# Layer-0 FFN of a four-layer Flamingo stack on one NeuronCore: the picked experts' first matrices gathered from HBM by indirect DMA instead of copied from a table in SBUF

## The chip, the cores and the metric

The kernel is one program on one core of one Trainium2 chip. The metric is the device time in microseconds of one execution; the time before is the median of 3 runs. The engines are named as in the profile: PE is TensorE (its weight loads are PEld), DVE is VectorE, ACT is ScalarE, POOL is GpSimd, SP is SyncE, which issues nearly all DMA transfers. A trailing q (DVEq, POOLq, SPq) marks the engine's own instruction queue.

## The reference

The input x is 16 batches of 256 tokens of 128 numbers, in fp32. Four layers follow each other, each a gated cross-attention and a gated FFN on layer-normed x. The change touches the FFN of layer 0, which picks two of eight experts for each batch (not for each token) from the mean of its tokens:

```python
def _L0_ffn_ref(x, gate_w, down_w, down_b, up_w, up_b):
    pooled = x.mean(axis=1)
    gate = jax.nn.softmax(pooled @ gate_w.T, axis=-1)
    top_w, top_i = jax.lax.top_k(gate, 2)
    top_w = top_w / (top_w.sum(axis=-1, keepdims=True) + 1e-08)
    Wd, bd, Wu, bu = down_w[top_i], down_b[top_i], up_w[top_i], up_b[top_i]
    h = gelu(einsum('bsd,bkcd->bksc', x, Wd) + bd[:, :, None, :])
    h = h * top_w[:, :, None, None]
    out = einsum('bksc,bkdc->bsd', h, Wu)
    return out + (top_w[:, :, None] * bu).sum(axis=1)[:, None, :]
...
x = x + jnp.tanh(g_ffn[0]) * _L0_ffn_ref(_layernorm(x, axis=-1), ...)
```

`pooled` is (16, 128), `down_w` is (8, 64, 128): one picked expert's first matrix is 64x128 fp32, 32 KB, and the 16 batches pick 32 of them.

## The kernel before

The program is written by hand, one instruction stream for each engine, tied together by semaphores: no scheduler moves anything, each engine executes its stream in order, and an instruction that waits holds back all behind it. x stays in SBUF for the whole kernel, as 32 tiles of 128 tokens. Attention is a software pipeline over the tiles (`attention(a)` gives a `step` for each engine; step t works on tiles t-3 to t+4). The opening steps -5, -4 and -3 of layer 1's attention are woven into the end of layer 0's FFN (`OPENING_BATCH = {12: -5, 13: -4, 14: -3}`).

**The routing of layer 0's FFN** is a chain of small DVE instructions (`route(...)`, lines 1071 to 1103), each waiting for the one before it by the semaphore `route_step`. The first index of the top two of each batch is kept in reversed form (8 minus the expert's number) in `T12 = lg[0:16, 3, 2:4]`, one batch to a partition. When the second pick is there (`ROUTE["picked0"]`), PE transposes the two columns into one row of `GV` (line 1572), behind `keep_busy(WARM_PICKS, ...)`, 14 matmuls of 128x128 on constants whose results nobody reads. DVE goes on with the gates (line 1090 to 1100), PE transposes the gates (line 1576), ACT copies them out (L807), PE makes the biases and the gates as columns for each batch, ACT copies those out (`w0col`, L809), and PE fills the wait with 6 more such matmuls (`WARM_COLUMNS`). At line 1103 DVE turns the row of picks into integers (`picks0`, `f0_idx`).

**The weights.** `wd_all` (128x512) holds all eight first matrices side by side, transposed so that the partition is the input channel d; SP loads it in line 415 early in the program. After `f0_idx`, POOL reads the picks of two batches into four registers (L618) and copies each picked 128x64 block into `wd_sel[:, b, :]` (L621), 32 copies, the two of a batch side by side: one matmul then handles both experts. DVE does the like for the second matrices, scaled by the gate (`up_weights`, L1117).

**The batches.** PE runs `up0(b)` (one matmul of 128x256, waits for `wd_made`, the weights of batch b) and `down0(b)` (three matmuls into PT). `up0` runs three batches ahead: up0(0), up0(1), up0(2), then for each b up0(b+3) and down0(b). ACT applies Gelu between the two (L816), DVE adds the result into x (`add0`, L1123). Behind the 32 copies, POOL's stream goes on with the opening of layer 1's attention: for tile 0 it waits for `mv_done`, which DVE gives behind `add0(12)`.

SP loads the attention weights of layer 2 (1.8 MB) in the middle of this stage, as soon as the values of layer 1 are made and `wq1` is copied.

Of the kernel before, what the change touches and what calls it, by code (L numbers as in the profile page):

```python
# [22 lines left out]
I32 = mybir.dt.int32  # L23
ALU = mybir.AluOpType
ACT = mybir.ActivationFunctionType
AX = mybir.AxisListType
ds = bass.ds

P = 128
BATCHES = 16  # L30
SEQ = 256
D = 128
# [6 lines left out]
EXPERTS = 8  # L39
BN = 64  # L40
# [35 lines left out]
class Signals:  # L76


    def __init__(self, sem):
# [70 lines left out]
        self.table_warm = sem("table_warm")  # L150
        self.wd_made = sem("wd_made")
        self.wu_made = sem("wu_made")
# [98 lines left out]
def flamingo_program(nc, io):  # L251
    with ExitStack() as ctx:
        def sb(name, shape, dt=F32):
            return ctx.enter_context(nc.sbuf_tensor(name, shape, dt))
# [10 lines left out]
        GV = ps("GV", [P, BANK])  # L265
# [30 lines left out]
        ident = sb("ident", [P, P])  # L296
# [37 lines left out]

        wd_all = sb("wd_all", [P, EXPERTS * BN])
        wd_sel = arena[:, 2048:4096].rearrange("p (b c) -> p b c", b=BATCHES)
# [64 lines left out]
        s = Signals(sem)  # L401
# [11 lines left out]
        def _(sp):  # L413
            def load(dst, src, sm):
                sp.dma_start(dst, src).then_inc(sm, 16)
# [46 lines left out]

            load(wd_all[:, :], io["L0_down_T"], s.f0_loaded)
            for n in range(2):
# [29 lines left out]
        def _(pool):  # L494
# [10 lines left out]
                      allow_small_or_imprecise_dtypes=True).then_inc(s.consts_made, 1)  # L505
            pool.wait_ge(s.consts_made, 9)
            pool.affine_select(out=ident[:, :], in_=ident[:, :], compare_op=ALU.not_equal, fill=1.0, base=0,
# [106 lines left out]
            pool.wait_ge(s.f0_loaded, F0)  # L614
            pool.wait_ge(s.f0_idx, 1)
            picked = [pool.alloc_register(f"down_pick{n}") for n in range(4)]
            for b in range(0, BATCHES, 2):
                pool.load(picked, picks0[0:1, b:b + 2, :].rearrange("p b k -> p (b k)"))  # L618
                for n in range(4):
                    e = pool.snap(picked[n], min_val=0, max_val=EXPERTS - 1)  # L620
                    ins = pool.tensor_copy(wd_sel[:, b + n // 2, BN * (n % 2):BN * (n % 2) + BN], wd_all[:, ds(e * BN, BN)])  # L621
                    if n % 2:
                        ins.then_inc(s.wd_made, 1)
            pool.wait_ge(s.m_evac, ATTN[2].mn0)
# [307 lines left out]
        def _(dve):  # L932
# [114 lines left out]
            def at(name):  # L1047

                assert ROUTE[name] == route_count[0], (name, route_count[0])

# [36 lines left out]
            route(dve.scalar_tensor_tensor(out=A0, in0=B0, scalar=second, in1=rv, op0=ALU.is_equal, op1=ALU.mult))  # L1087
            route(dve.tensor_reduce(T12[:, 1:2], A0, AX.X, ALU.max))
            at("picked0")
            route(dve.tensor_scalar(two, A0, T12[:, 1:2], None, ALU.is_equal))  # L1090
            dve.wait_ge(s.f0_exp, 2)
# [238 lines left out]
        def _(pe):  # L1330
# [239 lines left out]
            pe.wait_ge(s.route_step, ROUTE["picked0"])  # L1570
            for k in range(2):
                ins = pe.transpose(GV[0:1, 16 * k:16 * k + 16], lg[0:16, 3, 2 + k:3 + k], ident[0:16, 0:16])
            ins.then_inc(s.f0_picks_T, 1)
# [15 lines left out]
            def up0(b):  # L1589
                pe.wait_ge(s.wd_made, b + 1)  # L1590
                done(pe, s.act0_done, b - 4)
                mm(S[b // 2 % 2][:, BANK * (b % 2):BANK * (b % 2) + SEQ], wd_sel[:, b, :], xnT[:, SEQ * b:SEQ * b + SEQ]).then_inc(s.up0_done, 1)
# [140 lines left out]
SMALL = 11 * 16  # L1733
F0 = 5 * 16

WARM_UP, WARM_WEIGHTS, WARM_MN, WARM_DRAIN = 8, 2, 6, 2
WARM_POOLED, WARM_PICKS, WARM_COLUMNS = 4, 14, 6

ROUTE = {"pooled": 1, "exp0_ready": 3, "second0_ready": 8, "picked0": 10, "gates0": 20, "exp1_ready": 33, "exp2_ready": 42}
Q3 = {"inverses": 6, "weights": 10, "x_scale": 3, "h_scale": 3 + GROUPS + 2}  # L1740
# [38 lines left out]
```

## Time and profile before

| | |
|---|---|
| median of 3 runs | 1340.53 us (1340.12 to 1344.09) |
| the profiled execution | 1344.25 us, span from first to last instruction 1342.5 us |
| PE busy | 1242.9 us (93%) |
| DVE, ACT, POOL busy | 1044.0, 615.7, 562.1 us |
| mean granted TensorE clock | 0.965 |
| DMA | 15.36 MB, 11 GB/s over the span |
| layer 0's FFN, from the pooled means to `add0(15)` | 159.5 to 204.3 us of the span |

The profile counts an engine busy while an instruction of its own runs; a wait is put down to the engine and line that ended it. The granted clock is 1.00 at 2.4 GHz and 0.50 at 1.2 GHz. PE records of an fp32 matmul come in twos, so "x8" of `up0` is four matmuls.

### The profile page before, as it was taken

What the parts mean: (1) busy time and instruction counts of PE and PEld (TensorE: products, weight loads), DVE (VectorE), ACT (ScalarE), POOL (GpSimd) and SP (SyncE); (2) the same over time, 40 slices, a digit from 0 to 9 for tenths busy, and PEclk for the clock granted to TensorE, in tenths of its full rate; (3) what the DMA queues carried; (4) which work ended last, traced back from release to release, by engine and by line L of the source; (5) the groups of instructions that cost most, each with busy time, mean ns of one, the idle gap of its engine ahead of it and who ended that gap; (6) DMA issues with size and microseconds to landing.
All of it is one profiled execution on the core that took longest, in us unless ns stands there. A gap on an engine that the chain in (4) does not pass through costs nothing.

```text
span 1342.5 us, 25933 instructions
## 1 busy us (share of the span) xinstructions
PE 1242.9 (93%) x7491; PEld 912.2 (68%) x7492; DVE 1044.0 (78%) x2366; ACT 615.7 (46%) x1286; POOL 562.1 (42%) x1007
## 2 busy tenths in 40 slices
PE   7999788999998899999999998999999999999843
PEld 5666554666667788876766766888887666766612
DVE  3999556999996777777777775777776998888777
ACT  3555323555554322235555554322223555555475
POOL 2666324666675011315445543001001666666413
PEclk8999998999999899999999998999999999999975
DMA  8100200000000200000000000000000000000002
GB/s 215 49 0 1 55 2 1 1 0 0 0 1 1 55 1 0 0 0 1 1 0 0 0 1 1 1 1 0 0 0 1 1 1 0 0 0 1 1 0 63
DMA packets 24352, 15.36 MB, mean 11 GB/s; under 512 B 3833, under 2 KB 23074, under 8 KB 24290
## 3 DMA queue, kind: packets, MB, share of 16 engines
q1 hardware_dynamic: 24290, 14.59, 4.2%
q8 instruction: 32, 0.52, 0.2%
q14 instruction: 30, 0.25, 0.1%
HBM read 12.49 MB, written 2.10 MB: 11 GB/s over the span
## 4 chain that ended last, share of the span: by engine, by line
PE 74%; DVE 5%; ACT 5%; issue 4%; POOL 2%; ACTq 0%; DVEq 0%; POOLq 0%
PE S L1332 29%; PE OX L1332 14%; PE GV L1332 12%; PE PT L1332 11%; PE PT L1501 5%; ACT pT L780 1%; PE OX L1449 1%; POOL arena L565 1%; PE OX L1452 1%; ACT arena L760 1%; DVE arena L1275 1%; ACT moe_flat L893 1%; DVE zsum L1010 1%; POOL x L662 0%; DVE arena L1305 0%
## 5 line engine op out<-in xcount | busy, mean ns | idle before, releaser
L1332 PEld LDWEIGHTS OX<-arena,pT 128*128 128x128 f32 x1792 | 211.4, 193 | 55.0 <-issue 32.7
L565 POOL TENSOR_TENSOR arena<-arena,zinv 128x1024 f32<-128x1024 f32 (+1 forms) x128 | 215.9, 1687 | 75.5 <-DVE zinv L1014 75.4
L1332 PE MATMUL OX<-arena,pT 128*128 128x128 f32 x1792 | 231.8, 281 | 9.2 <-ACT pT L780 6.5
L831 ACT ACTIVATE arena<-S 128x512 f32<-128x512 f32 x144 | 86.0, 597 | 236.5 <-PE S L1332 236.5
L994 DVE TENSOR_REDUCE nmax<-S 128x16 f32<-128x1024 f32 (+1 forms) x128 | 139.7, 1092 | 47.6 <-PE S L1332 39.3
L1173 DVE TENSOR_TENSOR arena<-S,arena 128x512 f32<-128x512 f32 x144 | 99.6, 692 | 84.5 <-ACT arena L831 81.0
L1181 DVE SCALAR_TENSOR_TENSOR x<-PT,gate,x 128x128 f32 (+1 forms) x576 | 161.0, 343 | 2.2 <-PE PT L1332 2.2
L1332 PE MATMUL S<-arena,xT 128*128 (+1 forms) x320 | 161.0, 601 | 1.1 <-ACT arena L760 0.8
L537 POOL TENSOR_TENSOR rstd<-mv,eps 128x1 f32<-128x1 f32 x128 | 24.5, 192 | 315.1 <-DVE mv L996 315.1
L1003 DVE TENSOR_TENSOR arena<-S,nmax 128x1024 f32<-128x1024 f32 (+1 forms) x128 | 138.1, 1079 | 0.0
L1010 DVE TENSOR_REDUCE zsum<-arena 128x16 f32<-128x1024 f32 (+1 forms) x128 | 137.5, 1075 | 0.0
L1501 PEld LDWEIGHTS PT<-ident,arena 128*128 128x128 f32 x896 | 99.9, 142 | 51.8 <-issue 27.0
L1332 PE MATMUL S<-xh,w_low 128*128 (+1 forms) x288 | 126.1, 438 | 7.2 <-issue 7.2
L780 ACT ACTIVATE pT<-PT 128x512 f32<-128x512 f32 x224 | 123.6, 597 | 19.0 <-PE PT L1501 18.3
L1501 PE MATMUL PT<-ident,arena 128*128 128x128 f32 x896 | 125.2, 280 | 6.5 <-POOL arena L565 6.3
L727 ACT ACTIVATE arena<-arena 128x1024 f32<-128x1024 f32 (+1 forms) x128 | 120.7, 943 | 14.3 <-DVE arena L1003 14.3
L975 DVE TENSOR_SCALAR xn<-x,mv,rstd 128x128 f32 (+1 forms) x128 | 118.9, 929 | 8.0 <-POOL rstd L559 3.7
L1332 PE MATMUL GV<-N,ctx_b 97*64 97x512 f32 x448 | 122.1, 623 | 1.9 <-ACT arena L770 1.4
L586 POOL CAST xh<-xnT (+1 forms) x16 | 10.2, 636 | 252.5 <-PE S L1332 248.3
L1332 PE MATMUL S<-xh,w_high 128*128 (+1 forms) x288 | 114.2, 397 | 0.0
L1332 PE MATMUL S<-xl,w_high 128*128 (+1 forms) x288 | 113.4, 394 | 0.0
L770 ACT ACTIVATE arena<-GV 128x512 f32<-128x512 f32 x112 | 67.0, 598 | 83.0 <-PE GV L1332 82.9
(258 smaller groups left out, 2174.3 us busy)
## 6 DMA issues: line engine op xcount, KB each, us to landing
x<-in_x SPq DMA_DIRECT2D x4, 512.0 KB, 7.8
out<-x SPq DMA_DIRECT2D x8, 256.0 KB, 2.3
moe_flat<-in_L_ffn_w SPq DMA_DIRECT2D x3, 512.0 KB, 7.1
arena<-in_L_xattn_Wq SPq DMA_DIRECT2D x2, 512.0 KB
wo_in<-in_L_xattn_Wo SPq DMA_DIRECT2D x2, 512.0 KB
moe_flat<-in_L_up_T SPq DMA_DIRECT2D x2, 256.0 KB
moe<-in_L_ffn_we_gate SPq DMA_DIRECT2D x1, 512.0 KB, 5.3
moe<-in_L_ffn_we_up SPq DMA_DIRECT2D x1, 512.0 KB, 6.7
```

Source lines behind the costliest of these rows:

```text
L565: pool.tensor_tensor(pr, pr, z, ALU.mult).then_inc(s.probs_done, 1)
L727: act.activation(pr, pr, ACT.Exp).then_inc(s.exp_done, 1)
L780: act.activation(pT[:, r % 2, BANK * k:BANK * k + BANK], PT[:, BANK * k:BANK * k + BANK], ACT.Copy).then_inc(s.turned_evac, 1)
L831: act.activation(silu[:, e % 2, :], S[0][:, BANK * (e % 2):BANK * (e % 2) + BANK], ACT.Silu).then_inc(s.silu_done, 1)
L975: dve.tensor_scalar(xn2[:, r % 2, :], tokens(t - 2), mv2[:, q, 0:1], rstd2[:, q, 1:2], ALU.subtract, ALU.mult).then_inc(s.xn2_done, 1)
L994: dve.tensor_reduce(nmax[:, p, 0:H], sc, AX.X, ALU.max, negate=True).then_inc(s.max_done, 1)
L1003: dve.tensor_tensor(probs[:, j, 0:W].rearrange("p (h k) -> p h k", h=H), sc, nmax[:, p, 0:H].unsqueeze(2).to_broadcast([P, H, KEYS]), ALU. ...
L1010: dve.tensor_reduce(zsum[:, p, 0:H], probs[:, j, 0:W].rearrange("p (h k) -> p h k", h=H), AX.X, ALU.add).then_inc(s.sum_done, 1)
L1173: dve.tensor_tensor(hid[:, e % 2, :], S[1][:, BANK * (e % 2):BANK * (e % 2) + BANK], silu[:, e % 2, :], ALU.mult).then_inc(s.hid_done, 1)
L1181: ins = dve.scalar_tensor_tensor(out=xt, in0=PT[:, BANK * (e % 2) + P * q:BANK * (e % 2) + P * q + P], scalar=gate[:, ds(4 * g + q, 1), e: ...
L1332: return pe.matmul(out, lhsT, rhs, start=start, stop=stop)
L1501: ins = pe.transpose(PT[:, o:o + P], probs[:, r, o:o + P], ident[:, :])
```

## The change

The table `wd_all` and its load are gone. The first matrices lie in HBM as 1024 rows of 64 numbers (row 128*e + d), and each of the 32 copies on POOL becomes an indirect DMA from HBM: 128 rows of 256 bytes, one index for each partition, from a column of `rows0` (128x32, integers). To make `rows0`, DVE spreads the two columns of picks over diagonals (two instructions more in the routing chain), PE multiplies them by ones, which gives every partition all 32 picks (`GV[:, 32:64]`), and DVE turns them into row numbers with the partition's number (`row_base`, an iota made by POOL at the start). Each batch has a semaphore of its own, which both its transfers raise by 16.

```diff
-        self.wd_made = sem("wd_made")
+        self.wd_made = [sem(f"wd_made{b}") for b in range(BATCHES)]
+        self.f0_rows = sem("f0_rows")
+        self.f0_rows_T = sem("f0_rows_T")
...
-        wd_all = sb("wd_all", [P, EXPERTS * BN])
+        rows0 = sb("rows0", [P, 2 * BATCHES], I32)
+        row_base = sb("row_base", [P, 1])
...
-            load(wd_all[:, :], io["L0_down_T"], s.f0_loaded)
...
+            pool.iota(row_base[:, :], pattern=[[0, 1]], base=8 * P, channel_multiplier=1,
+                      allow_small_or_imprecise_dtypes=True).then_inc(s.consts_made, 1)
...
-            pool.wait_ge(s.f0_idx, 1)
-            picked = [pool.alloc_register(f"down_pick{n}") for n in range(4)]
-            for b in range(0, BATCHES, 2):
-                pool.load(picked, picks0[0:1, b:b + 2, :].rearrange("p b k -> p (b k)"))
-                for n in range(4):
-                    e = pool.snap(picked[n], min_val=0, max_val=EXPERTS - 1)
-                    ins = pool.tensor_copy(wd_sel[:, b + n // 2, BN * (n % 2):BN * (n % 2) + BN], wd_all[:, ds(e * BN, BN)])
-                    if n % 2:
-                        ins.then_inc(s.wd_made, 1)
+            pool.wait_ge(s.f0_rows, 1)
+            for b in range(BATCHES):
+                for k in range(2):
+                    n = BATCHES * k + b
+                    pool.indirect_dma_start(wd_sel[:, b, BN * k:BN * k + BN], None, io["L0_down_T"],
+                                            bass.IndirectOffsetOnAxis(ap=rows0[:, n:n + 1], axis=0)).then_inc(s.wd_made[b], 16)
...
+            for k in range(2):
+                route(dve.tensor_scalar(ra[0:16, 4 + 2 * k:6 + 2 * k, :].rearrange("p a e -> p (a e)"), ident[0:16, 0:16], T12[:, k:k + 1], None, ALU.mult))
             at("picked0")
+            dve.wait_ge(s.f0_rows_T, 1)
+            dve.tensor_scalar(rows0[:, :], GV[:, 32:64], -float(P), row_base[:, :], ALU.mult, ALU.add).then_inc(s.f0_rows, 1)
             route(dve.tensor_scalar(two, A0, T12[:, 1:2], None, ALU.is_equal))
...
             pe.wait_ge(s.route_step, ROUTE["picked0"])
             for k in range(2):
+                ins = mm(GV[:, 32 + 16 * k:48 + 16 * k], ones[0:16, :], ra[0:16, 4 + 2 * k:6 + 2 * k, :].rearrange("p a e -> p (a e)"))
+            ins.then_inc(s.f0_rows_T, 1)
+            pe.wait_ge(s.f0_rows, 1)
+            for k in range(2):
                 ins = pe.transpose(GV[0:1, 16 * k:16 * k + 16], lg[0:16, 3, 2 + k:3 + k], ident[0:16, 0:16])
...
-                pe.wait_ge(s.wd_made, b + 1)
+                pe.wait_ge(s.wd_made[b], 32)
```

`F0` goes from 5 * 16 to 4 * 16, and the later marks of `ROUTE` rise by two.

On POOL, between the copy of `wq1` and the opening of layer 1's attention, before the change (the first rows of 72; `TENSOR_LOAD` fills the registers, the `ISA` row stands ahead of each copy):

```order
L611 COPY M<-arena 128x128 [waits attn_w_loaded,g_done]
L618 TENSOR_LOAD picks [waits f0_idx,f0_loaded,out_done]
L620 ISA
L621 COPY arena<-wd_all 128x64
L620 ISA
L621 COPY arena<-wd_all 128x64
```

and after it:

```order
L615 COPY M<-arena 128x128 [waits attn_w_loaded,g_done]
L623 DMA arena<-in_L_down_T,rows 128x64 [waits f0_rows,f0_loaded,out_done]
L623 DMA arena<-in_L_down_T,rows 128x64 x31
L541 TENSOR_TENSOR rstd<-mv,eps 128x1 [waits mv_done,mn_done,m_evac]
L544 TENSOR_TENSOR rstd<-rstd,neg_half 128x1 [waits rstd_step]
```

The 32 transfers stand back to back in POOL's stream, and the opening of attention is behind all of them.

On DVE, the end of the routing chain before the change (`rb` and `oh` are scratch of the routing, `lg` holds `T12`):

```order
L1087 SCALAR_TENSOR_TENSOR rb<-rb,m,rev 16x8 [waits route_step]
L1088 TENSOR_REDUCE lg<-rb 16x1 [waits route_step]
L1090 TENSOR_SCALAR oh<-rb,lg 16x8 [waits route_step]
L1092 SCALAR_TENSOR_TENSOR r<-r 16x1 [waits f0_exp,route_step]
```

and after it:

```order
L1089 SCALAR_TENSOR_TENSOR rb<-rb,m,rev 16x8 [waits route_step]
L1090 TENSOR_REDUCE lg<-rb 16x1 [waits route_step]
L1092 TENSOR_SCALAR ra<-ident,lg 16x16 [waits route_step] x2
L1095 TENSOR_SCALAR rows<-GV,row_base 128x32 [waits f0_rows_T,route_step]
L1096 TENSOR_SCALAR oh<-rb,lg 16x8
L1098 SCALAR_TENSOR_TENSOR r<-r 16x1 [waits f0_exp,route_step]
```

Three instructions stand ahead of L1096 (`two`), and the third waits for PE.

On PE, after the change, from the matmuls that keep it busy to the transposes of the gates:

```order
L1338 MATMUL S<-ones 128x128 x14
L1338 MATMUL GV<-ra,ones 128x16 [waits route_step]
L1338 MATMUL GV<-ra,ones 128x16
L1582 MATMUL GV<-ident,lg 1x16 [waits f0_rows]
L1582 MATMUL GV<-ident,lg 1x16
L1586 MATMUL PT<-ident,oh 8x16 [waits route_step]
```

The first transpose of the picks now waits for `rows0`, where it waited for the picks alone.

## Rows read from the trace of the kernel before

**Rows 1.** The page: busy time of each engine.

```profile
PE 1242.9 (93%) x7491; PEld 912.2 (68%) x7492; DVE 1044.0 (78%) x2366; ACT 615.7 (46%) x1286; POOL 562.1 (42%) x1007
```

**Rows 2.** Chain that ended last, 168 to 195 us: start us, us, what.

```profile
170.94 1.26 PE PT L1332 x6
172.20 0.43 PE S L1332 x2
172.63 1.26 PE PT L1332 x6
173.90 0.43 PE S L1332 x2
...
191.33 1.28 PE PT L1332 x6
```

**Rows 3.** Timeline, PE: start us, us, engine line op, out<-in, count, idle before.

```profile
162.30 0.21 PE L1332 MATMUL OX<-gwT,pooled 128*16 128x8 f32 x2
162.44 3.39 PE L1332 MATMUL S<-ones 128*128 128x128 f32 x28
165.76 0.20 PE L1572 MATMUL GV<-ident,lg 16*1 16x16 f32 x2
...
169.04 1.89 PE L1332 MATMUL S<-xnT,arena 128*128 128x256 f32 x8
...
190.73 0.60 PE L1332 MATMUL S<-xnT,arena 128*128 128x256 f32 x2
```

**Rows 4.** Timeline, DVE, end of the routing chain.

```profile
162.62 0.15 DVE L1078 TENSOR_REDUCE m<-OX 16x1 f32<-16x8 f32 x1 [2.90 <-PE OX L1332]
...
164.49 0.22 DVE L1090 TENSOR_SCALAR oh<-rb,lg 16x8 f32<-16x8 f32 x1
...
166.21 0.48 DVE L1100 TENSOR_SCALAR ra<-ident,lg 16x16 f32<-16x16 f32 x2
166.72 0.18 DVE L1103 TENSOR_SCALAR picks<-GV 1x32 int32<-1x32 f32 x1
```

**Rows 5.** Timeline, POOL: the copies and what is behind them.

```profile
167.74 5.95 POOL L621 COPY arena<-wd_all 128x64 f32 x28 [10.98 <-DVE picks L1103]
174.07 0.77 POOL L621 COPY arena<-wd_all 128x64 f32 x4 [0.38 <-issue]
193.78 0.19 POOL L537 TENSOR_TENSOR rstd<-mv,eps 128x1 f32<-128x1 f32 x1 [18.94 <-DVE mv L996]
```

**Rows 6.** Groups by line and form, POOL: the copies.

```profile
L621 POOL COPY arena<-wd_all 128x64 f32 x32 | 6.3, 240 | 11.8 <-DVE picks L1103 11.0 <-issue 0.4
```

**Rows 7.** Timeline, SPq: how long the issue of a DMA takes.

```profile
12.60 2.69 SPq L415 DMA_DIRECT2D bo_in<-in_L_xattn_bo  x3
15.33 0.43 SPq L415 DMA_DIRECT2D ln_g<-in_L_xattn_ln_gamma  x1
15.81 0.43 SPq L415 DMA_DIRECT2D ln_b<-in_L_xattn_ln_beta  x1
...
25.21 1.71 SPq L415 DMA_DIRECT2D router_w<-in_L_ffn_router_w  x1
```

**Rows 8.** DMA issues: count, KB each, median us from issue to landing.

```profile
q_in<-in_L_ffn_w_up SPq DMA_DIRECT2D x1, 128.0 KB, 2.4
...
wvT<-in_L_v_T SPq DMA_DIRECT2D x1, 48.5 KB, 2.7
```

**Rows 9.** Windows: busy us of each engine, granted clock, DMA share, GB/s.

```profile
core 0: us, PE busy (x) PEld busy (x) DVE busy (x) ACT busy (x) POOL busy (x), PEclk, DMA share, GB/s
166.00:168.00 2.00, 0.97 (x14) 0.83 (x15) 0.80 (x4) 0.46 (x3) 0.26 (x2) 1.00 0.72 177
195.00:197.00 2.00, 0.31 (x1) 0.18 (x1) 1.93 (x3) 0.00 (x0) 1.65 (x2) 0.50 0.00 0
206.00:210.00 4.00, 3.35 (x8) 0.78 (x6) 1.78 (x3) 0.88 (x2) 0.31 (x2) 0.71 0.00 0
218.00:225.00 7.00, 5.73 (x34) 3.52 (x33) 6.18 (x11) 3.28 (x6) 3.53 (x5) 1.00 0.00 0
```

**Rows 10.** Timeline, PE, behind the last `up0`.

```profile
196.69 0.45 PE L1449 MATMUL OX<-ident,xn 128*128 128x128 f32 x1 [2.83 <-DVE xn L1023]
...
200.29 1.22 PE L1332 MATMUL PT<-arena 128*128 128x128 f32 x4
201.44 1.22 PE L1332 MATMUL PT<-upb_in,w0T 8*128 8x256 f32 x2
```

**Rows 11.** One line: POOL's all-reduce near the end, and what it waited for.

```profile
L650 POOLq MODIFY_POOL_CONFIG  x4: 11/11/11, 1271.6 to 1301.1; - x4
L650 POOL PARTITION_ALL_REDUCE gmax<-amax x2: 378/380/382, 1277.4 to 1314.9; - x2
...
issue: 5.7, 1
```

More of the change, by code:

```diff
@@ L505, in _ @@
                       allow_small_or_imprecise_dtypes=True).then_inc(s.consts_made, 1)
-            pool.wait_ge(s.consts_made, 9)
+            pool.iota(row_base[:, :], pattern=[[0, 1]], base=8 * P, channel_multiplier=1,
+                      allow_small_or_imprecise_dtypes=True).then_inc(s.consts_made, 1)
+            pool.wait_ge(s.consts_made, 10)
             pool.affine_select(out=ident[:, :], in_=ident[:, :], compare_op=ALU.not_equal, fill=1.0, base=0,
@@ L1733 @@
 SMALL = 11 * 16
-F0 = 5 * 16
+F0 = 4 * 16
 WARM_UP, WARM_WEIGHTS, WARM_MN, WARM_DRAIN = 8, 2, 6, 2
 WARM_POOLED, WARM_PICKS, WARM_COLUMNS = 4, 14, 6
-ROUTE = {"pooled": 1, "exp0_ready": 3, "second0_ready": 8, "picked0": 10, "gates0": 20, "exp1_ready": 33, "exp2_ready": 42}
+ROUTE = {"pooled": 1, "exp0_ready": 3, "second0_ready": 8, "picked0": 12, "gates0": 22, "exp1_ready": 35, "exp2_ready": 44}
 Q3 = {"inverses": 6, "weights": 10, "x_scale": 3, "h_scale": 3 + GROUPS + 2}
@@ L1765 @@
         "L1_v_T": np.concatenate([np.asarray(inputs["L1_xattn_wv"]), np.asarray(inputs["L1_xattn_bv"])[None, :]], axis=0).T,
-        "L0_down_T": np.asarray(inputs["L0_ffn_down_w"]).transpose(2, 0, 1).reshape(D, EXPERTS * BN),
+        "L0_down_T": np.asarray(inputs["L0_ffn_down_w"]).transpose(0, 2, 1).reshape(EXPERTS * D, BN),
         "L0_up_T": np.asarray(inputs["L0_ffn_up_w"]).transpose(2, 0, 1).reshape(BN, EXPERTS * D),
```

## The prediction
> **What bounds the kernel now.** I read the page first: PE is busy 93% of the span, POOL 42% [rows 1]. That share says nothing of this stage, so next the chain that ended last, cut to the stage: from 170.94 us on it is PE alone, in a beat of two pieces, six records into PT (`down0`) at 1.26 us and two into S (`up0`) at 0.43 us [rows 2]. The reader should see the regularity: 1.70 us for each batch, with no wait in between. PE sets the pace, and the copies on POOL don't: by POOL's timeline they run from 167.74 to 174.84 us, 7.1 us for all 32, and then POOL stands idle for 18.94 us until DVE gives it the statistics of tile 0 [rows 5]. A weight block for each batch every 0.44 us is far ahead of a PE that wants one every 1.70 us. The stage begins with the first `up0` at 169.04 and its last one, `up0(15)`, starts at 190.73 [rows 3]. Everything behind that (down0(12), the opening of layer 1) hangs on it. So the question is when `up0(15)` can start after the change.
>
> **The front of the stage.** DVE had the second pick at 164.49, where `two` began [rows 4]. Two instructions of 16x16 are put ahead of it; the pair of the same shape took 0.48 us [rows 4], so the diagonals are ready at about 165.0. PE isn't: its 14 matmuls on constants run from 162.44, and the next instruction began at 165.76 [rows 3]. The two products with ones go there; the two small transposes at that place took 0.20 us [rows 3]. PE to DVE costs 0.1 us (162.30 plus 0.21 on PE, 162.62 on DVE [rows 3, 4]). So `rows0` starts at 166.07, takes 0.18 like `picks0` [rows 4], and is there at 166.25.
>
> Two things follow. First, DVE stands still meanwhile, and the gates are queued behind it: `two` starts at 166.3 instead of 164.49, 1.8 us late. PE's transposes of the gates, ACT's copies, the gate columns and the 6 matmuls in front of `up0(0)` all wait for that chain, and up0(0) can't start before 169.04 + 1.8 = 170.8. Second, POOL gets its order earlier: the first gather starts at 166.35, where the first copy began at 167.74 [rows 5].
>
> The loads of registers on POOL and the copies, 7.1 us, are removed: worth nothing, since POOL waited 18.94 us behind them [rows 5]; that idle time is also the only cover for what replaces them. The load of `wd_all` goes: nothing, as it is on nobody's chain. The iota on POOL at the start is one small instruction among some fifteen, covered by PE's first matmuls: nothing.
>
> **The gathers.** All 32 stand back to back in POOL's stream. The trace of before has no transfer issued by POOL, so their price g (POOL's time for each) has to be bounded. From below: an issue on SP, done by hardware, 0.43 us, at a distance of 0.48 us from the next [rows 7]. From above: the longest issue of one transfer on SP, 1.71 us for `router_w` [rows 7]. The nearest row is `bo_in`: a transfer to 128 partitions, one short row each, 2.69 us for three, 0.90 each [rows 7]. POOL has to read 128 indices as well, and one pass of POOL over 128x64 takes 0.24 us [rows 6]. I add the two and take g = 1.1 us, 35.2 us for 32. This is halfway between the two ends, and I keep 0.48 and 1.71 for the range.
>
> The landing: a small load takes 2.4 to 2.7 us from issue to landing [rows 8], of which 0.43 is the issue; I take 2.0 us behind POOL's instruction (bounds 1.9 and 2.7). The first gathers also meet the weights of layer 2, which still kept the DMA engines busy at a share of 0.72 from 166 to 168 us [rows 9]; that delays the first blocks, not the last.
>
> The Trainium skill speaks against such a price: "DMA: Bandwidth & Descriptors", section "Anatomy of one DMA", says that most of the fixed 2 us of such a transfer is the receipt of the last byte and that many descriptors can be emitted before their cost shows. By that rule the gathers would overlap and g would be small; the result would be that of rival A below. No row here shows it either way. The same page's "Latency and other measured facts" gives about 1 us to the first byte for transfers generated on GpSimd, and with g = 1.0 the sum below would come to 9.6 us, an estimate by that page.
>
> **The sum.** Batch b has its two blocks at 166.35 + 2.2(b+1) + 2.0. Two blocks a batch need 2.2 us against PE's 1.70 [rows 2], so the bound passes from PE to POOL. up0(0) is ready at 170.55, just ahead of its 170.8. But PE runs `up0` three batches ahead, so down0(0) stands behind up0(3), which waits until 177.2. `up0(15)` can start at 166.35 + 35.2 + 2.0 = 203.55. Before, it started at 190.73 [rows 3]: **+12.8 us**. PE's 0.5 us of slack per batch can't be used, and its 1.8 us late start is inside the wait. Behind up0(15) the same things follow as before: POOL is free at 201.55, ahead of the statistics of tile 0 (they need add0(12), some 2 us behind up0(15)), so its opening isn't late on its own account. The layers after it are moved as a block.
>
> The profiled execution took 1344.25 us, 3.7 above the median of the runs shown; against itself it would be 1357.1. On the median, 1340.53 + 12.8 = **1353.3 us**.
>
> **The rivals.**
>
> *A: the gathers are hidden after all.* The issue on POOL is as cheap as on SP, 0.48 us [rows 7]. A batch then needs 0.96 us, PE keeps the bound at 1.70, and all that is left is the late start, 1.8 us: 1342.3, no change that can be measured. For it: the page's rule above, and POOL's idle 18.94 us. Against it: POOL computes addresses for 128 rows in software, and its cheapest pass over 128 partitions with a computed result costs half of that already. This decides where 166.35 + 32g + 2.0 falls below 194.7, so below g = 0.82. For a gain nothing speaks: PE's chain, not the weights, set the beat.
>
> *B: the gathers are dear.* g lies at the upper end, 1.71 us [rows 7]: 166.35 + 54.7 + 2.0 = 223.1, +32.3 us, 1372.8. With DVE instructions sharing SBUF with POOL, or indices costing more than a pass, g of 1.3 to 1.5 is well possible (+19.2 and +25.6). PE would then be idle for 1.3 us of each 3.0.
>
> *C: the clock falls.* Waiting for the first four blocks (170.8 to 177.2) PE has 0.43 us of work in each 2.2. Behind an idle stretch of 2.83 us [rows 10] the granted clock stood at 0.50, 1.2 GHz, and it had come back only between 206 and 210 [rows 9]. At that level six records into PT took 1.22 + 1.22 us [rows 10] instead of 1.26, so a batch costs about 3.3 us, more than the gathers' 2.2, and PE is the bound again. If it stayed so to the end: 177.2 + 12 x 3.3 = 216.8, +26.1, 1366.6. If it comes back within some batches, PE catches up at 0.5 us a batch and nothing is lost but perhaps 2.5 us, when the last batches still run at half clock (1355.8). PE at 82% was granted 1.00 from 218 to 225 [rows 9]; here it would be busy 77%.
>
> *D: POOL must first load code.* The all-reduce near the end came 5.7 us after a MODIFY_POOL_CONFIG in which it waited for nothing else [rows 11]. Were the first gather to pay this, the whole series is later: +18.5, 1359.0. The skill's "GPSIMD Engine Reference" names about 6 us for a first call to freshly loaded code; the trace's 5.7 agrees. Against it: the order of the changed kernel shows no such row ahead of the gathers.
>
> *E: the change doesn't do what it says*, the transfers being issued but something else holding `up0`: the waits are plain in PE's stream, 0.01.
>
> **How the numbers follow.** A measurement of this kernel tells 0.3%, 4.0 us, from no change. Forecast (g from 0.9 to 1.3, clock back soon) 0.60, at 1347 to 1360; A 0.07; B (g over 1.3) 0.17; C held to the end 0.10; D 0.05; E 0.01. The range takes in the forecast, C, D and B up to g of 1.5: 1346 to 1368, leaving out A and the dear end of B. Slower by over 0.3%: 0.92; within 0.3%: A with E, 0.07; faster 0.01.
>
> **What would show it.** Right: POOL's queue has 32 transfers back to back of 1.1 us each from 166.4 to about 201.6; in PE's timeline the beat of `up0` is 2.2 us with idle time before `up0`, released by a DMA; `two` (L1096) starts near 166.3; the last `up0` near 203.6. The stages behind keep their lengths. Wrong: the beat stays 1.70 (A), a gap of 6 us ahead of the first gather (D), or PE back to back at a granted clock of 0.50 (C).

## The result, and the profile of the changed kernel

| | before | changed |
|---|---|---|
| median, us | 1340.57 (4 runs) | 1386.91 (4 runs, 1385.95 to 1388.8) |
| profiled execution: span, us | 1342.5 | 1384.2 |
| mean granted clock | 0.965 | 0.941 |

The changed kernel is slower by 46.3 us; the ratio is 1.0328, 95% interval 1.0311 to 1.0345. The prediction was 1353.3 us: the direction was right, and the loss was more than three times the +12.8 forecast and lay outside the range (1346 to 1368).

The page first: PE's share fell, POOL's didn't. That is all it says of this stage.

```profile
PE 1264.4 (91%) x7496; PEld 922.5 (67%) x7496; DVE 1041.7 (75%) x2369; ACT 614.4 (44%) x1286; POOL 585.0 (42%) x1008
```

POOL's timeline answers to [rows 5]: first gathers and last one, and the first work behind them.

```profile
168.06 1.29 POOL L623 DMA_INDIRECT arena<-in_L_down_T,rows  x1 [10.96 <-DVE rows L1095]
169.66 0.94 POOL L623 DMA_INDIRECT arena<-in_L_down_T,rows  x1 [0.30 <-issue]
...
207.11 0.94 POOL L623 DMA_INDIRECT arena<-in_L_down_T,rows  x1 [0.30 <-issue]
239.44 0.18 POOL L541 TENSOR_TENSOR rstd<-mv,eps 128x1 f32<-128x1 f32 x1 [31.39 <-DVE mv L998]
```

The beat is 0.94 + 0.30 = 1.25 us, and the 32 gathers take 168.06 to 208.05. POOL then stands idle for 31.39 us. So POOL isn't what set the end, and PE's timeline has to be read (it answers to [rows 3]):

```profile
166.11 0.61 PE L1338 MATMUL GV<-ra,ones 16*128 16x16 f32 x4
...
169.38 0.21 PE L1586 MATMUL PT<-ident,oh 16*8 16x16 f32 x2 [2.04 <-DVE ra L1106]
...
173.18 1.06 PE L1338 MATMUL S<-xnT,arena 128*128 128x256 f32 x2
...
179.64 1.22 PE L1338 MATMUL S<-xnT,arena 128*128 128x256 f32 x2 [1.24 <-DMA arena<-in_L_down_T,rows]
...
192.42 1.06 PE L1338 MATMUL S<-xnT,arena 128*128 128x256 f32 x2
208.86 1.19 PE L1338 MATMUL PT<-upb_in,w0T 8*128 8x256 f32 x2 [15.38 <-issue]
...
213.84 1.19 PE L1338 MATMUL PT<-upb_in,w0T 8*128 8x256 f32 x2 [1.79 <-DVE x L1129]
...
234.90 1.06 PE L1338 MATMUL S<-xnT,arena 128*128 128x256 f32 x2
```

`up0(15)` starts at 234.90 instead of 190.73: +44.2 us, which is nearly the whole loss. (The two profiled spans differ by 41.7 us only: in the later layers the distance between the same instructions shrinks to some 40 us, first in the stretches of 200 us where the granted clock was 0.98 after and 0.97 before.) Three things are to be seen: `up0(3)` waits for its block until 179.64; from there a batch takes 3.15 us, not 1.70; and PE stands still for 15.38 and 1.79 us.

The windows give the clock: busy time of each engine, with PEclk behind it.

```profile
core 0: us, PE busy (x) PEld busy (x) DVE busy (x) ACT busy (x) POOL busy (x), PEclk, DMA share, GB/s
170.00:180.00 10.00, 7.03 (x27) 4.84 (x28) 2.84 (x10) 3.10 (x6) 7.56 (x9) 0.50 0.11 29
180.00:190.00 10.00, 10.00 (x26) 5.70 (x25) 1.67 (x5) 0.95 (x2) 7.56 (x9) 0.50 0.09 27
190.00:200.00 10.00, 3.48 (x9) 1.85 (x8) 0.29 (x2) 0.47 (x1) 7.56 (x9) 0.50 0.10 26
...
220.00:230.00 10.00, 10.00 (x26) 5.98 (x26) 3.25 (x11) 1.73 (x4) 0.00 (x0) 0.50 0.00 0
```

PE is at 1.2 GHz throughout, also where it is busy for 10.00 of 10.00 us. And DVE's timeline shows what PE stood still for:

```profile
189.39 0.42 DVE L1129 TENSOR_TENSOR x<-PT,x 128x256 f32<-128x256 f32 x1 [5.02 <-remote]
189.73 0.57 DVE L1123 TENSOR_SCALAR arena<-moe_flat,w0col 64x128 f32 x2
208.29 0.42 DVE L1129 TENSOR_TENSOR x<-PT,x 128x256 f32<-128x256 f32 x1 [17.99 <-remote]
...
213.27 0.42 DVE L1129 TENSOR_TENSOR x<-PT,x 128x256 f32<-128x256 f32 x1 [3.89 <-remote]
```

```profile
213.20 1.20 ACT L818 ACTIVATE arena<-S,w0col 128x256 f32<-128x256 f32 x3 [19.12 <-PE S L1338]
```

The `add0` at 208.29 is batch 2's. Its `down0(2)` was over on PE at about 189.5, so DVE had nothing to wait for and yet waited 17.99 us; "remote" means that the view finds no instruction near it in time that released it. ACT's gelu waited 19.12 us in the same way, until 213.20. PE's next `down0` needs that `add0` and stopped in turn. The signals from DVE to PE were prompt (208.71 to 208.86); those from PE were not. The lag outlasted the gathers: the last one was over at 208.05, `add0` of batch 2 came 0.24 us behind it, but ACT's three waiting gelus and `add0` of batch 3 (over on PE at about 192.5) came only at 213.2, and that is PE's second wait, of 1.79 us. The profile's ends of matmuls are modelled, so the trace can't tell whether only the signal was late or the end of the matmul itself. I call this **the stop**.

By sizes, at `up0(15)`: the gathers alone would have put it at 208.05 + 1.7 (landing, from an experiment below) = 209.75, +19.0. At half clock it is 179.64 + 12 x 3.15 = 217.4, another 7.7. The stop adds 15.38 + 1.79 = 17.2. The sum is 43.9 of the 44.2. No run has the gathers alone at full clock, so the first term is an estimate from these rows; experiment 14 below has the second, 38.0 us from `up0(3)` to `up0(15)` without a stop.

### The profile page after: what moved, and what is told of

Read it like the earlier page. It is cut to its first block and busy times, and to the rows that moved or that the text cites. A ratio compares the mean times of both kernels' runs of the same rounds, so it can differ in the third digit from the quotient of the medians.

```text
span 1384.2 us, 25906 instructions
## 1 busy us (share of the span) xinstructions
PE 1264.4 (91%) x7496; PEld 922.5 (67%) x7496; DVE 1041.7 (75%) x2369; ACT 614.4 (44%) x1286; POOL 585.0 (42%) x1008
## 3 DMA queue, kind: packets, MB, share of 16 engines
q0 software_dynamic: 1024, 1.05, 0.3%
```

## The experiments

**1. Gathers that nobody waits for.** Before, with gathers behind its copies:

```diff
+            for n in range(12):
+                pool.indirect_dma_start(spare[:, n, :], None, io["L0_down_T"]...,
+                                        bass.IndirectOffsetOnAxis(ap=row_i[:, 0:1], axis=0)).then_inc(s.spare, 16)
+            pool.wait_ge(s.spare, 12 * 16)
```

> The kernel before, with 12 indirect transfers of 128 rows added on POOL behind its 32 copies, with constant indices and into a spare part of the arena that nobody reads; POOL alone waits for them before its opening of layer 1. This is gathers beside the batches with nothing waiting for their data. The trace of the changed kernel has g = 1.25 us a gather, so 12 take 15.0 us behind the copies (about 174.9 to 190), and POOL was idle until 193.78 there. Theory 'stall' (gathers hold back the signals between PE, ACT and DVE while they run): DVE's add0 and ACT's gelu get late by several us at about 180 to 190, PE waits for them, and the time is 1345 to 1356 us. Theory 'clock alone' (the 15.4 us stop of PE in the changed kernel has another cause, such as the half clock or the order of waits): nothing moves in the batches, up0(15) stays at 190.7 within 0.5 us, and the time is that of before, 1340.5 within 1.5.

Measured: 1349.86 us against 1343.41, ratio 1.0050 (1.0032 to 1.0067). DVE's `add0` in this kernel, one per batch, should come every 1.70 us:

```profile
182.52 0.42 DVE L1135 TENSOR_TENSOR x<-PT,x 128x256 f32<-128x256 f32 x1 [0.74 <-PE PT L1344]
185.09 0.42 DVE L1135 TENSOR_TENSOR x<-PT,x 128x256 f32<-128x256 f32 x1 [1.47 <-PE PT L1344]
190.03 0.42 DVE L1135 TENSOR_TENSOR x<-PT,x 128x256 f32<-128x256 f32 x1 [3.99 <-remote]
```

The first gather was at 176.37; 9 us later PE's signals begin to lag, and this at a granted clock of 1.00 (until 191.4). No data of a gather was awaited. So gathers hold up PE's signals, and the half clock isn't needed for it.

**2. PE filled with narrow matmuls.**

```diff
             ins.then_inc(s.f0_picks_T, 1)
+            keep_busy(16, S[1])
...
             def up0(b):
+                keep_busy(16 if b < 4 else 7, OX)
                 pe.wait_ge(s.wd_made[b], 32)
```

> The changed kernel with PE filled by matmuls on constants into a bank nobody reads: 16 behind the transposes of the picks, 16 ahead of each of the first four up0 and 7 ahead of each later one, so that PE is not idle while it waits for gathers. At full clock one takes about 0.06 us, so the fillers fit into the wait of the gathers' beat of 2.5 us. Theory 'clock alone': the granted clock stays at 1.00 through the batches, the beat becomes the gathers' 2 x 1.25 = 2.5 us, up0(15) starts at about 168.06 + 32 x 1.25 + 1.2 = 209.3, and the time is 1340.5 + 18.6 = 1359 us (1355 to 1364). Theory 'stall': the clock is held, but PE still waits 10 to 16 us near 195 to 208 for a signal of ACT or DVE; up0(15) comes at 215 to 225 and the time is 1366 to 1376. If matmuls on constants do not hold the clock, it stays near 1387.

Measured: 1416.30 us, ratio 1.0539 (1.0517 to 1.0562), outside all three ranges. One filler took 0.24 us, not 0.06: 14 of them show as 28 records and took 3.39 us, and I had counted badly, so the fillers alone slow the batches. But the trace tells more. PE's timeline and windows, while POOL gathers:

```profile
193.26 0.37 PE L1338 MATMUL OX<-ones 128*128 128x128 f32 x1 [1.74 <-issue]
...
199.55 0.37 PE L1338 MATMUL OX<-ones 128*128 128x128 f32 x1 [1.52 <-issue]
201.67 0.37 PE L1338 MATMUL OX<-ones 128*128 128x128 f32 x1 [1.74 <-issue]
204.46 0.37 PE L1338 MATMUL OX<-ones 128*128 128x128 f32 x1 [2.42 <-issue]
```

```profile
190.00:200.00 10.00, 3.00 (x7) 1.74 (x7) 0.00 (x0) 0.00 (x0) 7.56 (x9) 0.50 0.09 27
...
220.00:230.00 10.00, 10.00 (x75) 8.62 (x75) 0.99 (x3) 1.42 (x3) 0.00 (x0) 1.00 0.00 1
```

These matmuls wait for no semaphore and send none, and still PE runs one record, half a matmul, in some 2 us (11 records from 190.43 to 210.06): beside the gathers PE itself is held back, not only its signals. The clock accounts for a factor of two, not for this. The two records of `up0(0)` started at 177.89 and 179.09, and ACT got its signal at 214.33. From 220 us on, with the gathers over, 75 records fit into 10 us.

**3. All gathers ahead of the batches.**

```diff
             pe.wait_ge(s.wq1_copied, 1)
+            for b in range(BATCHES):
+                pe.wait_ge(s.wd_made[b], 32)
```

> The changed kernel with PE waiting for all 32 gathers before up0(0): no batch overlaps a gather. The last block is there at about 209.3. Theory 'stall' (overlap of gathers with the batches is what stops PE): from there no wait of PE for DVE or ACT; up0(15) follows 12 batches after up0(3), at 1.70 us each at full clock about 230.5, at 3.15 us at half clock about 248. Time 1340.5 + 39.8 = 1380 or + 57 = 1398. Theory that the stop of 15 us has to do with the half clock and not with the gathers: a stop of over 5 us appears in this kernel too, behind the gathers, and the time is over 1400.

Measured: 1402.09 us (four runs, 1385.6 to 1404.9), ratio 1.0403 (1.0329 to 1.0477). There is no stop, so it needs the overlap. The last gather ended at 207.53 and `up0(0)` began at 209.23, 1.7 us behind it: the landing. And the clock:

```profile
212.00:250.00 38.00, 38.00 (x98) 22.39 (x97) 10.41 (x33) 5.69 (x12) 0.00 (x0) 0.50 0.00 0
```

38 us of batches without a gap, and the clock stays at 0.50. This is the case with half clock that the expectation named (1398 us), and it explains the profiled execution (1400.96). The run of 1385.6 has the highest mean granted clock of the four, 0.947 against 0.931 to 0.939; it has no profile.

**4. The front alone.** Before's copies behind the changed routing front, nobody gathers:

```diff
-                    pool.indirect_dma_start(wd_sel[:, b, ...], ..., rows0[:, n:n + 1] ...).then_inc(s.wd_made[b], 16)
+                    ins = pool.tensor_copy(wd_sel[:, b + n // 2, ...], wd_all[:, ds(e * BN, BN)])
```

> The changed kernel's routing front (the two diagonals, the products with ones, rows0, and PE and DVE waiting for one another there), but the blocks copied on POOL from the resident table by registers, as before; nobody reads rows0. It prices the front alone. By the prediction's step the front costs 1.8 us (2.5 by the changed kernel's trace, of which 0.35 lies ahead of it), up0(0) at 170.8 to 171.5, 1342.3 to 1343.0 us, if the clock is granted back as it was before. Theory 'the front starts the fall of the clock': PE is idle for 2.0 us ahead of the gates' transposes, the granted clock falls to 0.50 from 169 on, and the batches run at 3.15 us for as long as it is held: +10 to +24 us, 1350 to 1365. Theory 'the waits for the gathers start it': clock 1.00 through the batches, 1342 to 1344 us.

Measured: 1347.36 against 1343.41 us, ratio 1.0022 (1.0010 to 1.0034). That lies between the two ranges. The clock did fall, in the 1.91 us of idle PE ahead of the gates' transposes (at 168.8), but it came back at 175.7:

```profile
170.00:176.00 6.00, 5.98 (x28) 5.42 (x28) 3.08 (x10) 2.67 (x6) 5.18 (x26) 0.53 0.00 1
176.00:196.00 20.00, 20.00 (x95) 12.10 (x94) 10.42 (x33) 5.60 (x12) 1.26 (x7) 1.00 0.01 2
```

So the front starts the fall and costs about 4 us. Here the first three `up0` ran at half clock and the batches went on at 1.00 all the same. That the waits for gathers are what kept the clock down in the changed kernel is likely (in experiments 10 and 14 it came back in the front and fell again behind such waits), but not shown: in experiment 3 it stayed at 0.50 with no wait in the batches.

**5. Hardware transfers instead of gathers.** Before, without copies; SP fetches the picked blocks from memory, by registers, from the table in HBM as it lies before the change (rows of 256 bytes, 2 KB apart):

```diff
+                    for b in range(0, BATCHES, 2):
+                        sp.load(picked, picks0[0:1, b:b + 2, :].rearrange("p b k -> p (b k)"))
+                        for n in range(4):
+                            e = sp.snap(picked[n], min_val=0, max_val=EXPERTS - 1)
+                            sp.dma_start(wd_sel[:, b + n // 2, BN * (n % 2):BN * (n % 2) + BN],
+                                         io["L0_down_T"][:, ds(e * BN, BN)]).then_inc(s.wd_made[b + n // 2], 16)
```

> The kernel before, with the picked first matrices fetched from memory too, but issued by SP: SP loads the picks into registers, as POOL did, and issues 32 ordinary transfers of 128 rows whose source column comes from a register, in the place in its order behind layer 2's weights. No copies on POOL, no indirect transfer, no product with ones and no wait in the front. The nearest rows of SP: 0.48 us from issue to issue, 0.90 each for bo_in's 128 rows. Theory 'software transfers' (the delay of PE's signals comes from POOL writing its transfers' descriptors): no signal of PE comes late; with 0.48 a transfer PE keeps the pace and the time is 1341 to 1345; with 0.9 each, the last block is at about 167.7 + 29 + 2 = 199 us, +8 us, 1347 to 1352 (up to 1362 if the clock falls in the wait for the first blocks). Theory 'any small rows' (128 rows of 256 bytes from memory beside PE do it, whoever issues them): a stop of over 5 us in the batches here too, and 1365 or more.

Measured: ten runs, of which two took 1345.5 and 1346.0 us and eight 1363.9 to 1367.6; their median is 1365.2, but no single figure fits both. The mean granted clock of the two was 0.963 and 0.966, of the eight 0.944 to 0.950. (The table is still loaded in this kernel, but nobody reads it.) The profile is of one of the eight. It has no stop, and most of its loss is clock:

```profile
168.58 20.38 SPq L490 DMA_DIRECT2D arena<-in_L_down_T  x32
```

```profile
173.86 0.70 PE L1333 MATMUL S<-xnT,arena 128*128 128x256 f32 x2 [1.18 <-DMA arena<-in_L_down_T]
```

```profile
176.00:196.00 20.00, 20.00 (x52) 11.65 (x51) 5.66 (x18) 2.88 (x7) 0.00 (x0) 0.50 0.17 37
```

An issue costs 0.64 us, 1.27 a batch, so PE keeps the bound; `up0(3)` was only 4 us late. But idle stretches of 0.81, 0.34, 1.18 and 0.27 us ahead of the first four `up0` were followed by 0.50 from 175.6 to 230.2: 12 batches of 3.15 us instead of 1.70, `up0(15)` at 212.24, +21.5, of which the clock is some 17.

**6. Plain transfers issued by POOL.** The first experiment with

```diff
-                pool.indirect_dma_start(spare[:, n, :], None, ...)
+                pool.dma_start(spare[:, n, :], io["L0_down_T"][:, BN * (n % 8):BN * (n % 8) + BN]).then_inc(s.spare, 16)
```

> The first experiment's kernel with its 12 indirect transfers on POOL replaced by 12 plain ones of the same shape (128 rows of 256 bytes at fixed addresses, same place in POOL's order, same target). The indirect ones cost +6.5 us and made ACT's gelu and DVE's add0 4.5 us late at about 190. Theory 'software transfers': POOL spends about 1 us on each of these too, and PE's signals come late: 1344 to 1351. Theory 'the indices': plain transfers are cheap and disturb nobody, 1340 to 1343.5.

Measured: 1343.80 against 1343.19 us, ratio 1.0000 (0.9986 to 1.0014).

```profile
177.96 6.78 POOL L633 DMA_DIRECT2D arena<-in_L_down_T  x12 [1.06 <-issue]
```

0.57 us each, and every `add0` from 175.97 to 189.56 came 1.70 us behind the last. As many bytes to the same partitions, issued by the same engine, disturb nobody, and it isn't the DMA engines' load: from 180 to 184 us these transfers moved 0.25 MB at a mean share of 25.6%, the gathers of the first experiment 0.10 MB at 8.2%. Two things differ besides the form. The source rows lie 2 KB apart here and side by side there. And the series is over in 6.8 us, while in the first experiment the lag began only 9 us behind the first gather. Experiment 5 had 32 plain transfers over 20 us without a stop, but from SP. So the indirect form is the likely cause; a plain series of 15 us on POOL was not run.

**7. Gathers with pauses.** The first experiment with six gathers and, behind each,

```diff
+                pool.memset(spare[:, 6:16, :], 0.0).then_inc(s.pace, 1)
+                pool.wait_ge(s.pace, n + 1)
```

> The first experiment's kernel with half the gathers (6) and a memset of POOL with its own signal between any two (0.5 to 1 us), so that the series lasts nearly as long but POOL issues at about half the rate or a bit more. Theory 'backlog' (while a gather runs PE's signals drain more slowly than the batches make them, and the lag adds up): with pauses PE's signals can drain; no add0 is over 1 us late and the time is 1340 to 1343.5. Theory 'any gather stops the others for a fixed time': half the loss, 1343 to 1345, and late signals in this trace too.

Measured: 1343.84 against 1343.19 us, ratio 1.0000 (0.9988 to 1.0012), beat 1.88 us, no `add0` more than half a microsecond late. Six may have been too few, so the pauses were tried in the changed kernel too (10 and 14).

**8. PE filled with wide matmuls.**

```diff
+                fill_wide(3 if b < 4 else 1, OX)     # 128x384 each
```

> The changed kernel with PE filled as in the second experiment, but by matmuls of 384 columns: 3 in the front, 3 ahead of each of the first four up0, 1 ahead of each later one, so about the same busy time with a fifth of the added instructions (24 instead of 164). Theory 'backlog by instructions' (what is held up beside the gathers goes with the number of PE's instructions): PE is stopped for much less than in the filled kernel (1416 us), though for more than 10 us, since the batches' own 13 instructions remain; 1370 to 1395. Theory 'backlog by PE's busy time': as the filled kernel, 1405 to 1420. Theory that the stop was of the narrow fillers' own making and the clock is all else: 1359.

Measured: 1390.30 us, ratio 1.0337 (1.0308 to 1.0366).

```profile
170.00:186.00 16.00, 15.79 (x72) 10.49 (x72) 2.96 (x10) 3.27 (x7) 12.23 (x13) 1.00 0.09 28
```

```profile
196.62 1.19 PE L1338 MATMUL PT<-upb_in,w0T 8*128 8x256 f32 x2 [10.30 <-issue]
...
214.11 1.19 PE L1338 MATMUL PT<-upb_in,w0T 8*128 8x256 f32 x2 [13.02 <-ACT arena L818]
```

The clock stayed at 1.00 up to the stop, and the stop came all the same, 23.3 us in two parts. By its time the kernel falls to the theory of instructions (1370 to 1395), not to that of busy time. But between the first gather and the point where PE stuck stood 80 matmul records here, in 18 us; 87 in 10.5 us with the narrow fillers; 63 in 25.4 us in the changed kernel; and 56 in 11.7 us in the first experiment. Neither count is the same in all four, so what sets the moment of the stop stays open.

**9. Before, with its own idle stretch filled.**

```diff
+                    if a.l == 1 and isinstance(t, int) and t == -3:
+                        keep_busy(20, S[0])
                     if is_tile(t + 3):
                         pe.wait_ge(s.xn_done, a.tile0 + t + 4)
```

> The kernel before with 20 matmuls on constants (0.13 us each, 2.7 us) in PE's idle stretch of 2.83 us ahead of the transpose of tile 0 in layer 1's opening, so that the idle stretch behind which the granted clock fell to 0.50 (194.7 to 208.3 and again 211.7 to 215.2 us) is gone. Theory 'idle PE loses the clock': 1.00 is kept over this place, the pieces that took 1.22 us there take 0.7, and the 10 us of PE's work done at half clock take 5 less: 1335.5 us (1333 to 1338). Theory that the fall has another cause, or that the fillers only delay the transpose: 1340 to 1343.

Measured: 1342.54 against 1343.65 us, ratio 0.9996 (0.9986 to 1.0006), no difference. The 20 took 4.63 us, pushed the transpose back by some 1.5 us, and the clock fell later, from 202.7 to 209.4.

**10. The changed kernel with a pause behind each gather.**

```diff
+                    pool.memset(arena[:, 6528:7168], 0.0).then_inc(s.pace, 1)
+                    pool.wait_ge(s.pace, 2 * b + k + 1)
```

> The changed kernel with POOL pausing behind each gather by a memset of 128x640 with its own signal, which in the 6 spaced gathers made a beat of 1.88 us instead of 1.25 with no signal of PE late. It makes the gathers themselves slower: the last lands at about 168.1 + 32 x 1.88 + 1.2 = 229.5, where the changed kernel's up0(15) started at 234.9. Theory 'backlog' (gathers back to back, not their number, hold up PE's signals): no stop of PE other than for the blocks, up0(15) at 229.5 to 231, so about 4 us faster than the changed kernel in spite of 20 us more of POOL's time: 1379 to 1384. Theory 'number' (the six were too few to show it): the stop of 15 us is here too, 1395 or more.

Measured: 1381.72 us, ratio 1.0293 (1.0273 to 1.0313), where the changed kernel has 1.0328 (1.0311 to 1.0345).

```profile
184.56 1.22 PE L1341 MATMUL S<-xnT,arena 128*128 128x256 f32 x2 [2.59 <-DMA arena<-in_L_down_T,rows]
...
207.00 1.22 PE L1341 MATMUL S<-xnT,arena 128*128 128x256 f32 x2 [0.32 <-DMA arena<-in_L_down_T,rows]
...
229.30 1.22 PE L1341 MATMUL S<-xnT,arena 128*128 128x256 f32 x2
```

32 gathers, 20 us more of POOL's time, no stop, and faster. The number of gathers isn't the cause. The clock had come back at 176.1 and fell again at 179.5: a wait of 1.37 us for a block lay behind PE, and it was in one of 2.99 us.

**11. SP's transfers, with PE filled.**

```diff
             def up0(b):
+                if b < 4:
+                    keep_busy(6, OX)
```

> The kernel that fetches the picked matrices by SP's hardware transfers, with 6 matmuls on constants (0.8 us) ahead of each of the first four up0, where PE waited 0.81, 0.34, 1.18 and 0.27 us for blocks. Its ten runs without them fell into two groups: two at 1345.5 to 1346.0 and eight at 1364 to 1367.6, and in the profiled one (1365.0) the clock fell to 0.50 at 175.8 and stayed until 230.4 with PE never idle. Theory 'the half clock, once there, holds itself through the batches, and short idle stretches ahead of them start it': with PE filled all runs are in the fast group, 1343 to 1347 us, and the clock is 1.00 from 166 to 194 us. Theory that the two groups have another cause: both groups again.

Measured: six runs, 1348.9 to 1352.3, median 1351.41 against 1343.65 us, ratio 1.0065 (1.0050 to 1.0080). One group of times, clock 1.00 from 166 to 203.6; the time is above the 1343 to 1347 expected, because the fillers were too long (6 us in all).

**12. Before, with fewer fillers** (11 in place of 20).

> The kernel before with 11 matmuls on constants instead of the 20 of the last try ahead of the transpose of tile 0. In that run one took 0.23 us (4.63 for 20), not the 0.13 counted; two records make one matmul. The 20 delayed the transpose by 1.5 us and the clock still fell, later and for half as long (203.1 to 209.9). With 11 (2.5 us) the transpose isn't delayed. Theory 'the half clock is what the stretch costs': 1.5 to 4 us faster than before, ratio 0.997 to 0.999. Theory 'the fall only moves': no difference, ratio 0.999 to 1.001.

Measured: 1340.63 against 1342.51 us (12 and 22 runs), ratio 0.9984 (0.9971 to 0.9997). Windows over the opening, before and this kernel:

```profile
194.00:216.00 22.00, 16.11 (x35) 7.00 (x35) 8.47 (x14) 5.62 (x11) 6.13 (x9) 0.61 0.00 1
```

```profile
194.00:216.00 22.00, 17.61 (x65) 8.95 (x66) 10.96 (x18) 6.20 (x12) 6.98 (x12) 0.84 0.00 0
```

The median is 1.9 us below the kernel before, and the interval just leaves out no difference: a small gain, and the only one here.

**13. SP's transfers with 2 fillers each.**

> The kernel that fetches by SP's hardware transfers with 2 matmuls (0.5 us) instead of 6 (1.5 us each time) ahead of each of the first four up0. With 6 the clock held in the profiled run and all six runs were in one group, but up0(15) started at 197.8, since the fillers alone took 6 us: 1351.4. With 2 they fit into the waits for the blocks: up0(3) at about 174.9, up0(15) at 195.3, +4.6 us at most, 1343.5 to 1347.5 and one group of runs, if so much filling is enough to keep the clock; two groups, the slow one near 1365, if not.

Measured: 1347.92 against 1342.51 us (11 runs, 1344.5 to 1350.8), ratio 1.0038 (1.0025 to 1.0050), one group, 0.4 us above the range expected.

```profile
176.00:196.00 20.00, 20.00 (x96) 12.24 (x95) 10.84 (x34) 4.84 (x11) 0.00 (x0) 1.00 0.16 36
```

Beside experiment 5's row for the same 20 us: PE is busy for 20.00 us in both, at 1.00 with 96 records and at 0.50 with 52. One wait for a block was left in this profile, 1.89 us ahead of `up0(0)`, and the clock held over it. Half a microsecond of matmuls on constants ahead of each of four `up0` is worth 17 us against the eight slower runs of experiment 5, and nothing against its two faster ones. Of all kernels that fetch the picked matrices from memory this is the fastest, 39 us faster than the changed one.

**14. The changed kernel with a short pause** (memset of 128x128).

> The changed kernel with a short pause of POOL behind each gather (memset of 128x128 instead of 128x640, with its signal), beat about 1.45 us instead of 1.88 or 1.25. Theory 'backlog' with a rate: if the pause is long enough for PE's signals to drain, no stop; the half clock then sets the pace at 3.15 us a batch, up0(15) at about 181 + 37.8 = 219, 1368 us (1364 to 1374). If it is too short, a stop is back: between 1375 and 1390, and its length says how near.

Measured: 1372.44 us, ratio 1.0211 (1.0189 to 1.0232); the profiled execution took 1375.98.

```profile
169.34 0.22 POOL L626 MEMSET arena<- 128x128 f32 x1
169.84 0.96 POOL L624 DMA_INDIRECT arena<-in_L_down_T,rows  x1 [0.28 <-POOL arena L626]
```

```profile
180.00:214.00 34.00, 33.12 (x83) 19.45 (x84) 10.04 (x30) 5.08 (x11) 27.73 (x47) 0.50 0.08 24
```

```profile
218.88 1.06 PE L1341 MATMUL S<-xnT,arena 128*128 128x256 f32 x2
```

A beat of 1.44 us instead of 1.25 takes the whole stop away: no wait of PE in the batches from 180.88 on, 3.15 us a batch, `up0(15)` at 218.88. That is 16.0 us sooner than in the changed kernel, and the median is 14.5 us lower.

## Why the prediction was wrong, point by point

- *"The front of the stage"*, `two` at 166.3 and up0(0) at 170.8: `two` stood at 167.00, of which 0.35 was there ahead of it (PE's constants began at 162.79, not 162.44). The mechanism was right and 0.35 us short, since the products with ones took 0.61 us, not 0.20. up0(0) came at 173.18, because the clock had fallen and the columns' matmuls took 2.93 us instead of 1.60. I had costed the wait as time alone; experiment 4 shows that it also costs the clock.
- *"the first gather starts at 166.35"*: 168.06. rows0 was ready at 167.08, and POOL took another 1.0 us to start.
- *"take g = 1.1 us"*: 1.25, inside the bounds. *"The landing ... 2.0 us"*: 1.7 (experiment 3). Together with the start they make +19.0 at `up0(15)` instead of +12.8: 4.8 from g, 1.7 from the start, less 0.3. That forecast, rightly sized, is 1359.5 us (an estimate, as no run had the gathers alone), still within the range. In the trace of the changed kernel no first gather paid for code (D): it took 1.29 us, the others 0.94.
- The Trainium skill's rule against such a price ("DMA: Bandwidth & Descriptors", "Anatomy of one DMA") gave rival A. The gathers didn't overlap on POOL, and the measured 1.25 us decides. The estimate with g = 1.0 was nearer, but by luck: the page's figure is a time to the first byte, not POOL's time for each transfer.
- *"the bound passes from PE to POOL"* is the first step that failed. It leaned on *"C: the clock falls ... If it comes back within some batches, PE catches up"*, to which the forecast gave most of its weight. The clock fell at 168.8 and came back at 254.1, so at 3.15 us a batch PE, not POOL's 2.5, was the bound. I had read from [rows 9] that PE at 82% was granted 1.00, and took it that the batches would be granted the same. Experiments 3, 5 and 13 have the same batches, PE busy without a gap, at 1.00 throughout (13) or at 0.50 throughout (3 and 5); in experiment 4 they were entered at 0.50 and went on at 1.00, so half clock is held in some runs and not in all. C held to the end was priced at 216.8 for `up0(15)`; without the stop it would have been 217.4. A chance of 0.10 for it was the misjudgement, and the range ended close above its price.
- The second step that failed is a term that the sum doesn't have. The prediction calls POOL's idle time *"the only cover for what replaces them"* and charges the gathers to POOL's queue and the blocks' landing alone. No rival had POOL's transfers slow another engine down. That is the stop, 17.2 us at `up0(15)`; experiments 1, 3, 10 and 14 show it to come from gathers back to back beside PE's work.
- *"Behind up0(15) the same things follow as before"* and *"the layers after it are moved as a block"*: right, within some 4 us.

**What stays open.** Which resource the gathers and PE share isn't shown by any row; nor whether the pause works by the slower beat or because POOL then waits for a signal of its own. The Trainium skill ("SBUF — State Buffer", "Who interferes with whom") says, of SBUF's ports, that a DMA never contends with a compute engine. For the plain transfers of experiment 6 the trace agrees (ratio 1.0000). Beside the gathers of experiment 1 PE was held up (+6.5 us), so the sentence can't be taken as a rule for the time; whether a port of SBUF is what they share isn't shown. What ends a half clock stays open too: in experiment 4 it came back within 7 us, in experiment 3 it stayed through all 16 batches.

## What to carry to other kernels

A transfer that "only" uses idle POOL time can cost other engines: look at who else is late while it runs, and put a pause between indirect transfers, or use hardware transfers with an address from a register. A short wait of TensorE ahead of a long dense stretch needs two prices, the wait alone and the whole stretch at half clock: here it was some 4 us in experiment 4 and some 20 in eight of ten runs of experiment 5. Filling the wait (0.5 us at a time here) is cheap. And when a slower cause is removed, ask what would hold the stage next: here three causes lay over one another, and none alone explains the 46 us.

## What the runs showed of the hardware that was not expected

- Indirect transfers of 128 rows of 256 bytes, back to back at 1.25 us: PE's signals up to 21 us late in the changed kernel and 35 us with narrow fillers, and PE down to one record (half an fp32 matmul) in some 2 us. At 1.44 us, with a memset and its signal between two gathers, nothing of it.
- Plain transfers of the same shape on POOL: 0.57 us each; on SP with an address from a register: 0.64 us.
- Half clock held for 38 us and more under a PE that was busy for 100% of the time (212 to 250 us in experiment 3), and two groups of times 20 us apart for one kernel (experiment 5), with mean granted clocks of 0.963 and 0.966 in the faster and 0.944 to 0.950 in the slower.
